# Edge stage of a graph and expert layer: each block of edges gathered once into a ring of 28 blocks

## The reference

```
h = (xn @ W).reshape(N, HEADS, HEAD_DIM)
e = leaky_relu(a_src[src] + a_dst[dst], 0.2)
emax = segment_max(e, dst)
ee = exp(e - emax[dst])
denom = segment_sum(ee, dst)
msg = h[src] * (ee / denom[dst])
agg = segment_sum(msg, dst)
```

## Time and profile before

| what | value |
|---|---|
| median of 3 runs | 2294.04 us (2293.52 to 2295.35) |
| the profiled execution | 2291.67 us, span 2290.4 us |
| PE, DVE, ACT, POOL busy | 78%, 76%, 68%, 52% of the span |
| POOL's gathers of the edge stage | 880, 840.5 us busy |

### The profile page before, as it was taken

How to read it: one execution, slowest core, us unless ns; L and a number is a source line. 1 busy time by engine, 2 the same in 40 slices (tenths; PEclk the granted TensorE clock), 3 DMA queues, 4 the chain that set the end, 5 groups by cost and what they waited for, 6 DMA issues and landing times.

```text
span 2290.4 us, 43652 instructions
## 1 busy us (share of the span) xinstructions
PE 1796.5 (78%) x12962; PEld 1538.9 (67%) x12962; DVE 1745.3 (76%) x5414; ACT 1556.3 (68%) x3225; POOL 1184.8 (52%) x1168
## 2 busy tenths in 40 slices
PE   6537666676666677766666899999399999999998
PEld 4425545555545455555544788889399999999997
DVE  7349999899899899989998788887455555555554
ACT  3366777777677777676772787887377766666675
POOL 3377777777777777777770134445222222222223
PEclk9857777777777777777777999999699999999999
DMA  7867666767666667766664223322835356436432
GB/s 228 209 184 215 215 210 197 207 216 215 214 205 203 208 214 215 225 200 200 204 207 136 74 91 98 101 78 75 253 48 122 48 118 159 87 48 158 85 48 38
DMA packets 283231, 358.12 MB, mean 156 GB/s; under 512 B 118629, under 2 KB 227006, under 8 KB 280562
## 3 DMA queue, kind: packets, MB, share of 16 engines
q1 hardware_dynamic: 218578, 202.63, 28.7%
q0 software_dynamic: 63840, 151.61, 26.0%
q10 hardware_dynamic: 576, 1.09, 0.2%
HBM read 464.93 MB, written 95.79 MB: 245 GB/s over the span
## 4 chain that ended last, share of the span: by engine, by line
PE 46%; POOL 21%; issue 11%; DVE 11%; ACT 6%; DMA 4%; DVEq 0%; SPq 0%; POOLq 0%; ACTq 0%
POOL edge_mem L768 21%; PE bank L1156 8%; PE bank L1144 7%; PE bank L1145 7%; PE bank L1146 7%; PE bank L957 6%; PE bank L1155 4%; DMA edge_mem<-node_table,src_col 3%; ACT edge_mem L862 3%; DVE layer_rounded L1140 1%; PE bank L1153 1%; ACT edge_mem L868 1%; DVE edge_mem L1023 1%; PE bank L523 1%; PE bank L834 1%
## 5 line engine op out<-in xcount | busy, mean ns | idle before, releaser
L768 POOL DMA_INDIRECT edge_mem<-node_table,src_col x880 | 840.5, 955 | 277.2 <-issue 261.7
L957 PE MATMUL bank<-edge_mem 128*128 128x264 f32 x1760 | 524.1, 459 | 6.3 <-ACT edge_mem L897 3.3
L957 PEld LDWEIGHTS bank<-edge_mem 128*128 128x128 f32 x1760 | 382.9, 226 | 110.1 <-issue 26.3
L1886 POOL DMA_INDIRECT out<-expert_mem,slot_tok x112 | 174.4, 1557 | 488.4 <-DVE expert_mem L1823 468.5
L1873 ACT ACTIVATE expert_mem<-bank,par 128x256 f32<-128x256 f32 x448 | 221.8, 495 | 187.6 <-PE bank L1146 187.5
L1140 DVE TENSOR_TENSOR expert_rounded<-expert_mem,expert_rounded 128x512 fp32r<-128x512 f32 x280 | 193.6, 691 | 194.6 <-ACT expert_rounded L1873 121.9
L1023 DVE TENSOR_TENSOR edge_mem<-edge_mem,bank 128x1056 f32<-128x1056 f32 x385 | 293.9, 776 | 7.5 <-ACT bank L889 1.7
L1156 PE MATMUL bank<-expert_rounded 128*128 128x512 f32 x784 | 278.8, 395 | 0.0
L1144 PE MATMUL bank<-expert_rounded 128*128 128x256 f32 x896 | 254.6, 284 | 27.1 <-DVE expert_rounded L1140 27.1
L862 ACT ACTIVATE edge_mem<-iota,dst_col 128x128 bf16<-128x128 bf16 x880 | 262.8, 386 | 0.0
L1145 PE MATMUL bank<-expert_rounded 128*128 128x256 f32 x896 | 254.4, 284 | 0.0
(11 more groups left out here) (245 smaller groups left out, 4240.6 us busy)
## 6 DMA issues: line engine op xcount, KB each, us to landing
expert_rounded<-split_w SPq DMA_DIRECT2D x114, 2048.0 KB
edge_mem<-step_place SPq DMA_DIRECT2D x55, 512.0 KB, 5.4
split_w<-piece_hi SPq DMA_DIRECT2D x72, 256.0 KB, 4.8
split_w<-piece_lo SPq DMA_DIRECT2D x72, 256.0 KB, 6.0
piece_full<-in_L_ffn_W SPq DMA_DIRECT2D x64, 256.0 KB
expert_mem<-expert_rows SPq DMA_DIRECT2D x224, 64.0 KB, 2.8
edge_mem<-node_table,src_col POOLq DMA_INDIRECT x880
node_table<-win_mem SPq DMA_DIRECT2D x12, 544.0 KB, 4.4
```

Of the source, the lines that this page charges most:

```text
L768: pool.indirect_dma_start(gath[g % NGB][:, t, :], None, node_table, bass.IndirectOffsetOnAxis(ap=src_col[:, k, t % 2:t % 2 + 1], axis=0)). ...
L957: ins = pe.matmul(bank[4 + at % 3][:, 0:AGG], onehot[g % 2][:, 2 * k + j, :], gath[g % NGB][:, 2 * k + j, 0:AGG], start=(j == 0), stop=(j ...
```

## The change

Each block is gathered once: 782 gathers, into `ring`, which has room for RB = 28 blocks (block j lies at j mod 28). POOL goes through blocks in fours (a quad), and waits before each quad, from the eighth on, until the steps of the blocks that lay there are weighed; the number to wait for is loaded to a register from a table made in the node stage (`reuse_at`). The waits for PE are gone. A step finds its block's place by registers: block = step - window, and its remainder by 28, by a multiplication and a division by 65536 (`step_tile`). ACT loads the window word and four semaphore values (`landed_at`) a turn, waits for the four, and copies the scores of each step singly. DVE writes weighed messages to a buffer of their own, `message`, a step an instruction (the last two steps of a group a tile an instruction), and PE sums from there; scores come from `asrc`, of which there are two now. Source rows are loaded once a block by plain DMAs of SP, and no more gathered a step. A table of semaphore values is made on DVE. The first weights of the layer (`layer_w1`) now lie where messages lay, and are loaded after the last message. The core of the diff:

```diff
+    RB = 28
+    QUAD = 4
+    NQUAD = -(-NEB // QUAD)
...
-        gath = [part(i * GT * ROW, GT, ROW) for i in range(NGB)]
+        ring = part(0, 2 * RB, ROW)
+        message = part(2 * RB * ROW, GT, AGG)
...
+                    sp.dma_start(rows_s[0:min(P, NEB - c * P), c, :].bitcast(I32), src_rows[c * P:min((c + 1) * P, NEB), :]).then_inc(src_loaded, 16)
...
-                    pool.indirect_dma_start(rows_s[:, c, :].bitcast(I32), None, src_rows, at).then_inc(rows_gathered, 16)
...
+                dve.memset(rows_s[:, :, :], 0.0).then_inc(src_cleared, 1)
...
+        def step_tile(words, g, k):
+            block = nc.s_assert_within(g * GS + k - step_window(words, k), 0, NEB - 1, skip_runtime_bounds_check_because="a step's block")
+            at = (block - ((block * (-(-65536 // RB))) >> 16) * RB) * 2
+            return nc.s_assert_within(at, 0, 2 * RB - 2, skip_runtime_bounds_check_because="a block's place in the ring")
...
-                    if g >= 2 and t % QUART == 0:
-                        if t == QUART:
-                            pool.wait_ge(asrc_turned, g - 1)
-                        if t == 2 * QUART:
-                            pool.wait_ge(cand_turned, g - 1)
-                        if t == 3 * QUART:
-                            pool.wait_ge(maxima_made, g - 1)
-                    if g >= NGB and t % QUART == 0:
-                        pool.wait_ge(summed, GS * (g - NGB) + (GS // 2 if t < 2 * QUART else GS))
...
+                if q >= RB // QUAD:
+                    done = pool.value_load(reuse_at[0:1, q - RB // QUAD + 1:q - RB // QUAD + 2], min_val=1, max_val=NSTEP)
+                    pool.wait_ge(weighted, done)
+                    pool.sem_inc(quad_free, 1)
+                    pool.wait_ge(quad_free, q - RB // QUAD + 1)
+                if q >= QUAD:
+                    pool.wait_ge(gathered[q % QUAD], 32 * QUAD * (q // QUAD))
+                for j in range(q * QUAD, min((q + 1) * QUAD, NEB)):
...
-                    act.wait_ge(gathered[n % NGB], 16 * GT * (n // NGB + 1))
-                    if n >= 1:
-                        act.wait_ge(asrc_turned, n)
-                    act.copy(asrc[:, :, :, :], gb[:, :, :, AGG:ROW].rearrange("p k j h -> p j k h")).then_inc(asrc_ready, 1)
+                    words = act.value_load(win_word[0:1, n:n + 1], min_val=0, max_val=(1 << 27) - 1)
...
+                        landed = [act.value_load(landed_at[0:1, n, i:i + 1], min_val=1, max_val=32 * QUAD * NQUAD) for i in range(QUAD)]
+                        for i in range(QUAD):
+                            act.wait_ge(gathered[i], landed[i])
+                    if n >= 2:
+                        act.wait_ge(asrc_turned, n - 1)
+                        act.wait_ge(scored, n - 1)
+                    for k in range(GS):
+                        t = step_tile(words, n, k)
+                        ins = act.copy(asrc[n % 2][:, :, k, :], ring[:, bass.ds(t, 2), AGG:ROW])
+                    ins.then_inc(asrc_ready, 1)
...
-                dve.tensor_tensor(rows_, rows_, wgt[:, r, :].unsqueeze(3).to_broadcast([P, end - first_, HEADS, HC]), ALU.mult).then_inc(weighted, 1)
...
+                t = step_tile(word(g), g, k)
+                return dve.tensor_tensor(message[:, 2 * k + first_:2 * k + end, :].rearrange("p t (h c) -> p t h c", c=HC),
...
+            def early_messages(g, m):
+                for k in (2 * m, 2 * m + 1):
+                    weigh(g, k, 0, 2).then_inc(weighted, 1)
...
+            sp.wait_ge(weighted, GS * NG)
+            sp.wait_ge(summed, GS * (NG - 1) + GS // 2)
+            sp.dma_start(layer_w1[:, 0:2 * WSZ].bitcast(F32), split_w[E, 0, :, :]).then_inc(w1_loaded, 16)
```

More of the change, by code:

```diff
@@ L145, in build @@
         assert o + 3 * D <= OH0 and KC * P == D
[L147 to L151, removed]
+        src_col = sb1("src_col", [P, NEB, 2], I32)
+        dst_col = sb1("dst_col", [P, NSTEP, 2])
+        last_col = sb1("last_col", [P, NSTEP, 2])
         win_word = sb1("win_word", [1, NG], I32)
@@ L171, in build @@
         src_f = rows_i[:, :, :].bitcast(F32)
+        WS0 = PB0 + 1600 + 4 * NK * EB + 16 + NK * EB // 2
+        win_row, win_delta, win_shift = (part(WS0 + i * NSTEP, NSTEP).bitcast(I32) for i in range(3))
+        win_row = win_row[0:1, :]
+        win_delta, win_shift = (t[0:1, :].rearrange("o (g k) -> o g k", k=GS) for t in (win_delta, win_shift))
+        assert WS0 + 3 * NSTEP <= OT0 + 2 * GT * P - P
         count = sb1("count", [P, 4 * 5])
@@ L181, in build @@
         seg_max = sb1("seg_max", [HEADS * GS, EB])
-        asrc = sb1("asrc", [P, 2, GS, HEADS])
+        asrc = [sb1(f"asrc{i}", [P, 2, GS, HEADS]) for i in range(2)]
         cand = sb1("cand", [P, 2, GS, 3, HEADS + 1], BF16)
@@ L189, in build @@
         rest = sb1("rest", [P, GS, 2 * HEADS])
-        shift0 = sb1("shift0", [P, GS, HEADS])
+        shift0 = rest[:, :, 0:HEADS]
         absent = sb1("absent", [P, GS])
@@ L552, in build @@
         src_rows = src.rearrange("(b e) -> b e", e=EB)
+        NKB = -(-NEB // P)
         COLS = (7, 8, 10)
@@ L844, in edges_act @@
             act.wait_ge(cols_copied, 2 * 3)
+            act.wait_ge(words_made, 3)
             act.wait_ge(new_ready, 1)
@@ L951, in sum_step @@
                 pe.wait_ge(oh_wide, g + 1)
-            if k == 0 or piece_of(2 * k + 1) != piece_of(2 * k - 1):
-                pe.wait_ge(weighted, NM * g + piece_of(2 * k + 1) + 1)
+            if k % 2 == 0 and k < EARLY:
+                pe.wait_ge(weighted, GS * g + k + 2)
+            if k >= EARLY:
+                pe.wait_ge(weighted, GS * g + k + 1)
             if at >= 3:
@@ L956, in sum_step @@
             for j in range(2):
-                ins = pe.matmul(bank[4 + at % 3][:, 0:AGG], onehot[g % 2][:, 2 * k + j, :], gath[g % NGB][:, 2 * k + j, 0:AGG],
+                ins = pe.matmul(bank[4 + at % 3][:, 0:AGG], onehot[g % 2][:, 2 * k + j, :], message[:, 2 * k + j, :],
                                 start=(j == 0), stop=(j == 1))
@@ L1036, in edges_dve @@
                         if k < QUART:
-                            messages(p, 3 + k)
+                            late_message(p, k)
                             next(small, None)
@@ L1075, in edges_dve @@
                 if 0 <= g < NG:
-                    messages(g, 0)
+                    early_messages(g, 0)
                 if n < NG:
@@ L1080, in edges_dve @@
                 if 0 <= g < NG:
-                    messages(g, 1)
-                    messages(g, 2)
+                    early_messages(g, 1)
+                    early_messages(g, 2)
         w1_loaded, w2_loaded, layer_vectors = sem("w1_loaded"), sem("w2_loaded"), sem("layer_vectors")
@@ L1159, in x1_stored, with blocks_done @@
             eng.wait_ge(x1_written[b % 2], 16 * (b // 2 + 1))
+        assert 2 * WSZ <= BUF and 3 * BUF + 2 * WSZ <= 2 * RB * ROW + GS * AGG
+        def blocks_done(i):
+            last = max(j for j in range(NEB - RB, NEB) if i * GS <= j % RB < (i + 1) * GS)
+            return min(last + NT, GS * NG - 1) + 1
         def layer_sp():
             pieces_stored(sp, N_PIECES)
-            sp.wait_ge(summed, GS * (NG - 3))
-            sp.dma_start(layer_w1[:, 0:2 * WSZ].bitcast(F32), split_w[E, 0, :, :]).then_inc(w1_loaded, 16)
-            sp.wait_ge(summed, GS * (NG - 2))
+            sp.wait_ge(weighted, blocks_done(0))
             sp.dma_start(layer_w2[:, 0:2 * WSZ].bitcast(F32), split_w[E, 1, :, :]).then_inc(w2_loaded, 16)
-            sp.wait_ge(summed, GS * (NG - 1))
+            sp.wait_ge(weighted, blocks_done(1))
             sp.dma_start(g2_row, ln2_g.unsqueeze(0).to_broadcast([P, D])).then_inc(layer_vectors, 16)
```

96 lines of the change are left out of this document (62 added, 34 removed).

## The result

The changed kernel takes 2324.03 us (median of 4 runs, 2323.16 to 2325.05); the kernel before, run beside it, 2294.17. The ratio is 1.0132, 95% interval 1.0119 to 1.0145: slower by 30 us, 6 us above the forecast of 2318. The profiled run of after took 2324.22 us, with 2323.0 of span against 2290.4.

A forecast was written before the change was run, and what follows sets the result against it. POOL was taken to bound the edge stage, with DVE close behind; after the change, ACT's and DVE's chains. Turns +25, node stage -2, tail +1 sum to +24: 2318 us; forecast range 2299 to 2365, 8 in 10 from 2264 to 2390.

The forecast's parts named there:

- New turn: Edge stage: one pass over a group of eight steps takes 20.6 us, +0.47, over 54 turns +25 us.
- 0.15 for the interlock: Edge stage: ACT's 20.45 and DVE's 20.2 us chains hold each other twice a turn, adding 0.15 us, a choice.
- 16 x 1.25: Edge stage before: sixteen gathers 1.25 us apart make POOL's turn 20.0 us, so POOL bounds the stage.
- the ring does not stall them: POOL's gathers: with 28 blocks of ring, a group's gathers are let go about one turn before they are wanted.
- stretch: ACT between L897 and L862: five loads, six waits and eight copies take 7.85 us where 7.89 are spent now.
- the split of the messages: DVE's early messages, six of 528 elements for three of 1056: 3.7 us for 3.5, +0.2 a turn.
- The registers: DVE's address work: +0.3 us at the first message behind the weights wait, +0.4 at two late messages, each turn.
- Node stage -2: Node stage: four small gathers go, clearing source rows and small table operations come; -2 us, between -4 and +2.
- Weights of the layer: First layer weights, asked for at the last message, land in 10.0 us; some 8 us of cover remain.
- Tail +1: After the last turn: +1 us for that turn's extra work.
- Faster: Rival: register instructions hide, ACT's turn falls to 19.6 us, DVE's to 19.5; kernel 2272 us; chance 0.22.
- Dear registers: Rival: ACT's loads at 638 ns or more, division 0.3 us or above; turn 23.3, kernel 2465, half-way 2390; chance 0.19.

The follow-up runs named there:

- before_few: The kernel before with the last four of each group's 16 gathers replaced by one plain transfer of 512 fixed node-table rows: 2242.1 us.
- before_nostops: The kernel before without POOL's three waits for PE ahead of the second, third and fourth quarter of each group's gathers: 2294.6 us.
- dve_early: The changed kernel with DVE's ring places of a group's first and last two steps worked out under the scan, ACT unchanged: 2315.8 us.
- act_early: The changed kernel with ACT's five register loads and eight ring places worked out a turn ahead, under its own activations: 2316.9 us.
- both_early: The changed kernel with both ACT's loads and places a turn ahead and DVE's places worked out under the scan: 2282.6 us.

## Why the prediction was right, and where its steps were not

**Direction and size.** 30 us slower where the sum had +24. POOL stops being the bound, and register work takes its place, as told; but it is DVE's, where the forecast had ACT's as the longer. New turn: 20.6 forecast, 20.61 measured. That this fits so well is luck: the forecast is ACT's 20.45 and 0.15 for the interlock, the measured turn is that of DVE, which the forecast had at 20.2. In the span, ordinary turns gave 23.4 us for 25, the ring 5.7 for nothing, the start +2.7 for -2, the tail 0.8 for 1.

**POOL.** Right: 16 x 1.25 was the bound (before_few), its stops cost nothing (before_nostops), and gathers still stand 1.25 us apart. Waits now name DVE's messages. Wrong: "the ring does not stall them". It held POOL for over 5 us twelve times, and once, in the groups with most blocks, it cost a turn 5.7 us. What the step left out is that a stop of 7.71 us can't be won back while every group brings near eight blocks, each 2.5 us of POOL, 20.0 us in a turn of 20.6. A reading was off too: of the 308.8 us in the earlier trace rows the first copy has 29.8, so the others wait 5.2 us and not 5.7; the bound does not hang on it.

**ACT.** Right in each part: loads of 275 ns for 270 taken, copies 0.61 us apart on the mean for 0.61, stretch 7.4 to 7.9 in most turns for 7.85. The turn of dve_early, 20.43 for 20.45, has 0.3 us of waiting for DVE in it. But ACT was not the bound.

**DVE.** This is the term that was mis-sized: 20.2 forecast, 20.6 measured, above ACT. Its old turn of 19.3 was right (19.37) and the split of the messages too (0.2 of busy time for +0.2). The registers were not: 0.7 forecast; in the rows 27.8 us of idle in some 22 turns at L1069, 1.27 each, for 0.12 in before_few, 1.15 more. In the turn shown it is 0.71 us at the first message for 0.3, with the wait for the weights, and 0.65 at the two late ones for 0.4. The prediction priced the long fused instruction at 0.16 for both engines. On ACT its longest is 233 ns, on DVE 315; a plain move has 29 and 36. The Trainium skill (Advanced Engine Details and Errata, section "Clock Domains") states that DVE's sequencer runs at 0.96 GHz and those of the other engines at 1.2, so that the same number of cycles takes DVE 25% longer. The moves agree, 36 / 29 = 1.24; the longest fused ones stand at 1.35, so the clocks are not all of it.

**The 0.15 for interlocking chains** has nothing behind it in this kernel: act_early took 5 us out of ACT's stretch and left the turn where it was. In dve_early the two do wait for each other, 0.5 and 0.3 us a turn; what that costs, no run shows.

**The rest.** Node stage -2: the first gather starts at 94.5 us, 1.9 earlier by POOL's times. Not in the sum: in the first group nothing lies ahead of the copies, so all eight are seen; the first L907 starts 4.66 us after the first copy, 0.2 before, and the first turn comes 2.7 us late in spite of the gather. Weights of the layer: hidden, as told. They were asked for at 1282.13 and landed in 8.3 us; the first matmul at 1300.29 waits, as in the earlier trace rows, for DVE:

```profile
1300.29 0.79 PE L1202 MATMUL bank<-layer_rounded,layer_w 128*128 128x512 f32 x1 [2.91 <-DVE layer_rounded L1198]
```

Tail +1: 0.8.

**The rivals.** Faster was not impossible, only not so written: both_early is what that rival described, registers hidden behind other work, at 2283 for its 2272. "POOL that cost nothing would give 43 us, no more" was close: in before_few the turns gave 45, of the 54 in all. Dear registers: no load on ACT in the stage is near 638 ns at the median. By the floor of about 600 ns that the Trainium skill states (DMA: Bandwidth & Descriptors, section "Latency and other measured facts") ACT's turn would have been 22.1; the trace disagrees, 275 ns.

## What to carry to other kernels

Replacing work on the engine that bounds a stage by register work on the two next to it pays only as far as that work lies under something: here each dynamic place left its engine idle for 0.3 to 0.4 us where the instruction behind it was short. Place such work under a long instruction, a turn ahead if need be. Two engines 0.2 us apart have to be relieved together: here the one alone gave 0.01 us a turn, the other 0.18, both 0.66. Before joining small instructions, look at whose address work they cover.

## What the chip showed that I had not expected

Eight copies of 128x16 took 0.94 us together with their places ready and stood 0.59 us apart without, for 0.20 us of each. The same register work costs more on DVE than on ACT (moves of 36 and 29 ns). A plain transfer of 512 rows held POOL for 0.82 us where four indirect ones take 5.0 with their gaps (before_few):

```profile
L772 POOL DMA_DIRECT2D edge_mem<-node_table x55 | 44.8, 815 | 0.1
```
